# Macaron block on eight cores: two LayerNorm stages evacuate their transposes on ScalarE instead of VectorE, and the first one runs without stagger

## What is computed

```
x = x + 0.5 * ffn(layernorm(x), w_gate, w_up, w_down)     # FFN1, hidden 3072, int32 weights / 127
x = x + attn(layernorm(x), Wq, Wk, Wv, Wo, omega, ...)    # causal kernel attention, inner layernorm, W1/W2 with relu
x = x + 0.5 * ffn(layernorm(x), w_gate, w_up, w_down)     # FFN2, same weights as FFN1
ffn(h)       = (silu(h @ wg.T) * (h @ wu.T)) @ wd.T
layernorm(x) = (x - mean(x)) / sqrt(var(x) + 1e-5)        # over the 1024 features
```

## Time and profile before

| | |
|---|---|
| time, median of three runs | 2457.94 us (2456.14 to 2459.2) |
| time of the profiled execution | 2458.69 us |
| its spans, fastest and slowest core | 2432.0 us (core 4), 2457.1 us (core 1) |
| TensorE matmul busy | 1957.6 us, 80% of the span |
| VectorE busy | 766.9 us, 31% |
| ScalarE busy | 579.1 us, 24% |
| GpSimd busy | 65.6 us, 3% |
| granted TensorE clock, mean of core 1 | 0.906 of full speed |

### The profile page before, as it was taken

How to read it: one execution, slowest core, us unless ns; L and a number is a source line. 1 busy time by engine, 2 the same in 40 slices (tenths; PEclk the granted TensorE clock), 3 DMA queues, 4 the chain that set the end, 5 groups by cost and what they waited for, 6 DMA issues and landing times.

```text
span 2457.1 us, 31397 instructions; the slowest of 8 cores (2432.0 to 2457.1 us)
## 1 busy us (share of the span) xinstructions
PE 1957.6 (80%) x10480; PEld 957.0 (39%) x10480; DVE 766.9 (31%) x1813; ACT 579.1 (24%) x1382; POOL 65.6 (3%) x113
## 2 busy tenths in 40 slices
PE   0799969999403489997673789898995899969999
PEld 0344424444201255654332344444443444424444
DVE  3512211212400058888536413131225211112211
ACT  2311111111000068888426000000004311001100
POOL 1000010000000000000000000000001000000000
PEclk9999989999656699996596899999997899989999
DMA  9963135430699900000100333333336151163431
GB/s 221 118 81 79 52 43 89 75 103 1 70 116 115 119 27 19 19 11 2 35 1 1 124 134 137 138 137 124 136 136 121 23 97 61 43 103 52 103 137 52
DMA packets 81817, 199.90 MB, mean 81 GB/s; under 512 B 3840, under 2 KB 49152, under 8 KB 73472
## 3 DMA queue, kind: packets, MB, share of 16 engines
q0 software_dynamic: 42096, 82.39, 24.3%
q1 hardware_dynamic: 37264, 107.11, 13.0%
q10 hardware_dynamic: 2304, 8.39, 1.0%
HBM read 271.87 MB, written 37.75 MB: 126 GB/s over the span
## 4 chain that ended last, share of the span: by engine, by line
PE 67%; DMA 11%; another core or an unknown queue 6%; DVE 6%; ACT 4%; issue 4%; SPq 1%; DVEq 0%; POOL 0%; ACTq 0%; POOLq 0%; PEldq 0%
PE p L395 14%; PE p L415 14%; PE p L1137 9%; PE p L1169 9%; PE p L471 5%; PE p L477 5%; PE p L639 4%; DMA BufC<-Wq_bf 2%; DMA BufC<-Wk_bf 2%; DMA BufC<-Wv_bf 2%; PE p L674 2%; DMA BufC<-wuT_i 2%; DMA BufC<-wdT_bf 1%; DMA b2t_s<-b2t 1%
## 5 line engine op out<-in xcount | busy, mean ns | idle before, releaser
L395 PE MATMUL p<-fmA,BufC 128*128 128x512 bf16 x1536 | 369.1, 383 | 49.3 <-DMA BufC<-wuT_i 49.3
L415 PE MATMUL p<-fmA,BufC 128*128 128x512 bf16 x1536 | 364.8, 380 | 0.0
L431 DVE SCALAR_TENSOR_TENSOR actB<-p,tmpF 128x512 bf16<-128x512 f32 x192 | 132.9, 692 | 588.1 <-PE p L415 584.3
L471 PE MATMUL p<-BufC,actB 128*128 128x512 bf16 x768 | 293.0, 382 | 16.7 <-DMA BufC<-wdT_bf 12.7
L477 PE MATMUL p<-BufC,actB 128*128 128x512 bf16 x768 | 293.0, 382 | 0.0
L426 ACT ACTIVATE tmpF<-p 128x512 f32<-128x512 f32 x192 | 114.6, 597 | 647.1 <-PE p L395 647.1
L395 PEld LDWEIGHTS p<-fmA,BufC 128*128 128x128 bf16 x1536 | 151.1, 99 | 234.7 <-issue 57.0
L1137 PE MATMUL p<-fmA,BufC 128*128 128x512 bf16 x1024 | 224.3, 382 | 8.1 <-DMA BufC<-W_bf 8.1
L1169 PE MATMUL p<-actB,BufC 128*128 128x512 bf16 x1024 | 226.2, 379 | 4.3 <-DVE actB L1147 4.3
L415 PEld LDWEIGHTS p<-fmA,BufC 128*128 128x128 bf16 x1536 | 151.0, 98 | 183.6 <-issue 4.1
L639 PE MATMUL p<-fmA,BufC 128*128 128x512 bf16 x512 | 127.5, 394 | 116.3 <-DMA BufC<-Wq_bf 69.5
(11 more groups left out here) (109 smaller groups left out, 1731.2 us busy)
## 6 DMA issues: line engine op xcount, KB each, us to landing
BufC<-W_bf SPq DMA_DIRECT2D x64, 1024.0 KB, 5.8
BufC<-wgT_i POOLq DMA_DIRECT2D x32, 768.0 KB, 16.7
BufC<-wuT_i POOLq DMA_DIRECT2D x32, 768.0 KB, 19.8
W_bf<-W_sw POOLq DMA_DIRECT2D x2, 8192.0 KB, 142.5
BufC<-wdT_bf SPq DMA_DIRECT2D x4, 3072.0 KB, 12.4
BufC<-wdT_bf SPq DMA_DIRECT2D x12, 1024.0 KB, 10.7
wdT_bf<-wdT_i POOLq DMA_DIRECT2D x1, 6144.0 KB, 120.6
x_tm<-xin ACTq DMA_DIRECT2D x8, 512.0 KB, 21.3
```

The lines of the kernel that those rows point to most:

```text
L395: e.matmul(pg[pi][:, 0:512], BufC[:, wg_off + k * 768 + hcl * 128: wg_off + k * 768 + (hcl + 1) * 128], fmA[:, k * 2048 + tt0 + tsl * 512: ...
L415: e.matmul(pu[pi][:, 0:512], BufC[:, wu_off + k * 768 + hcl * 128: wu_off + k * 768 + (hcl + 1) * 128], fmA[:, k * 2048 + tt0 + tsl * 512: ...
L431: e.scalar_tensor_tensor(actB[:, hc * 1024 + tsl * 512: hc * 1024 + (tsl + 1) * 512], pu[pi][:, 0:512], INV127, tmpF[:, pi * 512:(pi + 1) ...
L471: e.matmul(da[:, 0:512], actB[:, hc * 1024 + tl * 128: hc * 1024 + (tl + 1) * 128], BufC[:, hc * 1024: hc * 1024 + 512], start=(hc == 0), ...
```

## The change

LN1: the call loses `pipe_stagger=2` and `pipe_ev_vec=True`, so all statistics come first on VectorE and on ScalarE, and the evacuation goes to ScalarE. LN2: the evacuation goes to ScalarE, and the casts of W1 and W2 wait for ScalarE's counter (`eS`) instead of VectorE's. The argument `pipe_ev_vec` is gone, which renumbers the lines behind it by one or two. LN3 keeps its arguments and its order.

```diff
@@ emit_outer_ln
-                          pipe_chunks=True, pipe_stagger=False,
-                          pipe_ev_vec=False):
+                          pipe_chunks=True, pipe_stagger=False):
...
-                if pipe and not pipe_ev_vec:
+                if pipe:
                     ev_tag[c] = (eS, op("scalar", lambda e, dst=dst, src=src:
                                         e.copy(dst, src),
                                         waits=[(eT, tr_tag[c])], inc=eS))
@@ the call for LN1
-        ln1_ev = emit_outer_ln(1e-5, pipe=True, pipe_stagger=2,
-                               pipe_ev_vec=True)
+        ln1_ev = emit_outer_ln(1e-5, pipe=True)
@@ LN2
-                ln2_ev[c] = (eV, op("vector", lambda e, dst=dst, src=src:
-                                    e.tensor_copy(dst, src), waits=[(eT, tt)], inc=eV))
+                ln2_ev[c] = (eS, op("scalar", lambda e, dst=dst, src=src:
+                                    e.copy(dst, src), waits=[(eT, tt)], inc=eS))
...
             cast_w1 = dma("gpsimd", cw1, W1_bf[:, :, :, :], W1_sw,
-                          waits=[(eV, t_ln2)], max_dma_last_dim=8192)
+                          waits=[(eS, t_ln2)], max_dma_last_dim=8192)
             cast_w2 = dma("gpsimd", cw2, W2_bf[:, :, :, :], W2_sw,
-                          waits=[(eV, t_ln2)], max_dma_last_dim=8192)
+                          waits=[(eS, t_ln2)], max_dma_last_dim=8192)
```

## The result

| | before | after |
|---|---|---|
| median of 8 runs each | 2457.38 us | 2431.88 us |
| ratio of the two, 95% interval | | 0.9897 (0.9885 to 0.9909) |
| profiled execution: time, span | 2458.69, 2457.1 us | 2431.43, 2429.9 us |
| the same, fastest core | 2432.0 us | 2405.6 us |
| TensorE matmul busy | 1957.6 us | 1935.4 us |

A forecast was written before the change was run, and what follows sets the result against it. The prediction took LN1's wait for the last small table, with twelve chunks of statistics left behind it, as the bound; LN2 was covered. 2458.69 us minus 21.1 us gives 2437.6 us, as median 2437 us, range 2432 to 2443 us.

The forecast's parts named there:

- The first copy at 49.0 us: LN1: the first evacuation starts at 49.0 us, after ScalarE's last statistics, with the tables landed at 47.53 us.
- The round of 2.28 us: LN1's loop from transposes to evacuation and back: 2.28 us for two chunks, 1.14 us for one, from LN3's end.
- the lower bound which I had kept as luck: LN1's loop at ScalarE's back-to-back copy pace, 0.91 us a chunk; would give 2.8 us more over six rounds.
- FFN1 from the start on: FFN1 moves up with its start at 65.6 us; its first quarter's matmuls keep their 43.0 us.
- The third quarter's weights: FFN1: last transfer lands at 149.3 us, wanted at 150.9 us, so no stall, with 1.6 us to spare.
- Rival (a): FFN1's third-quarter weights come late, costing 2.5 us: 2439.5 us, still faster; chance 0.06.
- The sum: Whole kernel: profiled 2458.69 us minus LN1's 21.1 us is 2437.6 us; median 2437 us, 0.86% faster.
- The cap of 22.7 us: FFN1: with weights landing at 149.3 us, starting before 64.0 us gains nothing, so at most 22.7 us is saved.
- Value 0: LN2: its evacuations end 24.4 us sooner, hidden by the wait for the slab of Wq, so worth nothing.
- Rival (c): LN2: earlier casts of W1 and W2 delay those of Wq, Wk, Wv by 48.9 us: 2486 us, slower; chance 0.04.
- Rival (b): LN1's loop does not overlap and keeps 2.82 us a chunk: gain 0.9 us, 2457 us, no change; chance 0.03.
- a loss of 10.9 us: Estimate by the skill's cycle rule (0.66 us VectorE, 1.00 us ScalarE) for moving 32 copies; the prediction did not adopt it.

The follow-up runs named there:

- the last kernel: Changed kernel with identity loaded first, LN1 staggered by one chunk, copies alternating between ScalarE and VectorE, down projection's cast in halves; against before: ratio 0.9866, median 2429.09 us.
- LN2 alone: Kernel before with only LN2's evacuation moved to ScalarE and the casts of W1 and W2 waiting for it; ratio to before 0.9985.
- the order alone: Kernel before with LN1's stagger removed but its evacuation still on VectorE, LN2 as before; ratio to before 1.0013, core mean +5.2 us.

## Why the prediction was right, step by step

**The first copy at 49.0 us.** It came at 49.71 us. The last group of x let its first sum start at 40.51 us (forecast 40.2 us), the squares of chunk 12 started at 42.09 us (41.8 us), and the price of a chunk on ScalarE held: those of chunk 15 started at 47.54 us, three steps of 1.82 us later. ScalarE's last statistic ended at 49.45 us. The last 0.26 us ScalarE waited for the transposes, since the tables landed at 48.61 us on this core and not at 47.53 us; the two bounds had come almost together.

**The round of 2.28 us.** It was 2.30 us for the first two rounds (the first from 49.71 to 52.01), and from then on mostly 1.89 us (56.19 to 58.07). The step that was mis-sized is this one. The rows of LN3's end show the loop only with transposes of 1.01 us, at a granted clock of 0.50; here eight transposes fell from 1.01 to 0.61 us by the seventh group, and the loop ran at 0.94 us a chunk, close to the 0.91 us at which ScalarE takes copies back to back. That is near the lower bound which I had kept as luck. Its effect on FFN1's start is 64.83 instead of 65.6 us: the later first copy took back 0.7 us of the 1.5 us gained.

**FFN1 from the start on.** I took its first quarter from before, 43.0 us. It takes 106.77 - 64.83 = 41.9 us now. Before, the first eight matmuls took 2.74 us; now the first seven recorded take 1.67 us. On the cores with all eight recorded they take 1.89 us, and in the mean the first quarter is shorter by 1.0 us. No term held that.

**The third quarter's weights.** Forecast: last transfer at 149.3 us, wanted 150.9 us. Measured: 108.99 + 40.31 = 149.3 us, wanted at 149.43 - 0.92 = 148.5 us. The queue was in order and as fast as worked out; the need came 2.4 us sooner. The two points above make some 1.8 us of it. The rest is a reading: I took the time of need from the issue on GpSimd at 171.17 us, but TensorE's first matmul of that quarter stands 0.7 us before it in the trace before:

```profile
170.46 1.89 PE L395 MATMUL p<-fmA,BufC 128*128 128x512 bf16 x8
```

Rival (a), late weights, came true, on this core at 0.9 us instead of 2.5 us, on the others at up to 2.7 us. The sum had put it at nothing, with 1.6 us to spare. The cap of 22.7 us for FFN1, in its end, holds: the mean of the cores is 22.8 us by the middle of FFN1. In the last kernel, with the cast split, it is 27.3 us there. That is also why an earlier start beyond this brings little unless the cast of the down projection moves.

**LN2.** Value 0 was nearly right: alone it gives 1.6 +- 0.5 us. Its copies were 0.98 us apart in the mean, not 1.14 us, for the same reason as in LN1. Rival (c), that the earlier casts of W1 and W2 hold up those of Wq, Wk and Wv, is refuted: from issue of the Wq cast to its slab the cores take 58.0 us in the mean after, 59.0 us before, and 58.9 us with LN2 alone. Where the 1.6 us arise I could not locate; the cores differ by more than that in every stretch.

**Rival (b), no overlap.** It did not come true in the changed kernel, but with the order alone it does: 2.8 to 3.0 us a chunk and FFN1 at 93 us. Its cause is then one list for step 2 and copy, and it is the other engine that avoids it.

**The sum.** Forecast -21.1 us. Measured on the means of the cores: 22.9 us at FFN1's start, +1.0 for its first quarter, -1.1 for the weights, +2.9 from its middle to the end, of which LN2's edit is 1.6 us by its own experiment; the remaining 1.3 us is within the scatter of the cores and stays open. So the mechanism in LN1 was right and its size nearly so. That the total still fell at the edge of the range is partly luck, since the sum had put the 2.9 us behind FFN1's middle at nothing. The cycle counts of the Trainium skill, "VectorE: DVE Perf Modes", section "The TRN2 errata — SBUF-src ops pay a fixed extra latency per instruction", from which the prediction estimated a loss of 10.9 us for 32 copies, describe their lengths (measured 1.01 against 0.69 us) and not the time of the kernel: ScalarE's busy time rose by 30 us, and the end came 25.5 us earlier.

## What to carry to other kernels

When an engine waits at the start for a transfer, ask of every other engine's list whether something that could run stands behind something that waits for that engine; and look first at the transfer itself. Here its place in the queue and its shared semaphore were nearly the whole cost: one small transfer, moved ahead and given a semaphore of its own, did in the old order nearly what the reordering did. Two edits that give little or do harm alone can be one edit: an in-order list stops at its first blocked instruction, and the gain comes only when no list is left with one ahead of work that could run.

## What the runs showed of the hardware

**Eight transposes took 1.01 or 0.61 us, and before FFN1 the granted clock does not tell which.** Stretches of TensorE: the time window, its length, matmul busy time with the count, the granted clock as a share of full speed, and the DMA share and rate. After, then before:

```profile
48.00:53.00 5.00, 3.76 (x32) 1.00 1.12 172
53.00:55.00 2.00, 1.74 (x16) 1.00 1.10 167
55.00:65.00 10.00, 6.24 (x81) 1.00 1.11 160
...
609.00:613.00 4.00, 3.58 (x32) 0.50 0.00 0
616.00:626.00 10.00, 5.65 (x76) 1.00 0.94 104
```

```profile
0.00:47.00 47.00, 0.00 (x0) 1.00 0.98 239
60.00:86.00 26.00, 10.20 (x82) 1.00 1.04 132
...
627.00:676.00 49.00, 16.41 (x130) 0.54 0.82 89
...
1905.00:1917.00 12.00, 5.17 (x45) 0.50 0.39 72
```

In LN2 after, the two lengths go with the two levels of the granted clock: eight transposes take 1.01 us from 609 to 613 us at 0.50 (1.2 GHz) and 0.61 us from 616 us on at 1.00 (2.4 GHz). TensorE had run nothing but these transposes in between, 3.58 of 4.0 us from 609 us on; so transposes alone were followed by the rise. In LN2 before it was busy 16.41 of 49 us, and the mean stayed at 0.54. The end of LN3, from which the prediction took its loop, stands at 0.50.

Up to FFN1 the column reads 1.00 in every row, also from 0 to 47 us, where TensorE had run nothing at all, and also where the lengths are those that go with 0.50 elsewhere. After, they fall from 1.01 to 0.61 us when TensorE had been busy 3.76 of 5.0 us. Before, it was busy 10.2 of 26 us, the transposes stayed at 1.01 us to the last, and the first eight matmuls of FFN1 took 2.74 us; on the slowest cores of the other kernels whose transposes stayed at 1.01 us they took 2.5 to 3.6 us. That TensorE was at its lower level there is my reading from the lengths; the column does not show it. At the start of a trace go by the length of equal instructions.

**A small transfer behind large ones.** After, `b2t` (4 KB) is issued at 15.60 us and lands 32.9 us later, near 48.6 us, behind 8 MB of x; the identity, 32 KB, issued at 6.11 us, lands 35.6 us later. And the same x loads, half of them issued 3.1 us later, delivered their first group 12.5 us later. At that time GpSimd's casts are in their queue too; that these took the place is my reading, not shown.
